# First attention of a two-layer block: scores and maxima as products of 64 rows, the two heads of a pair in turn on the two halves of TensorE's rows

## The reference, cut to what matters

```python
q = query @ w_q                     # layer-normed x, 256 -> 16 heads of 64
k, v = jnp.split(context @ w_kv, 2, axis=-1)
scores = jnp.einsum('bhqd,bhkd->bhqk', q, k) * 64 ** -0.5
attn = jax.nn.softmax(scores, axis=-1)
out = jnp.einsum('bhqk,bhkd->bhqd', attn, v)
return out @ w_out + b_out          # heads side by side, 1024 -> 256
```

## Time and profile before

| What | Value |
|---|---|
| Median of 3 runs | 3254.3 us |
| The profiled execution, its own time | 3254.05 us |
| Its span | 3252.2 us |
| TensorE (PE) busy | 3098.2 us, 95% |
| VectorE (DVE) busy | 2258.3 us, 69% |
| ScalarE (ACT) busy | 1646.5 us, 51% |
| GpSimd (POOL) busy | 1313.5 us, 40% |
| First attention | to about 1900 us of the span |

### The profile page before, as it was taken

How to read it: one execution, slowest core, us unless ns; L and a number is a source line. 1 busy time by engine, 2 the same in 40 slices (tenths; PEclk the granted TensorE clock), 3 DMA queues, 4 the chain that set the end, 5 groups by cost and what they waited for, 6 DMA issues and landing times. The chain is left out here.

```text
span 3252.2 us, 40235 instructions
## 1 busy us (share of the span) xinstructions
PE 3098.2 (95%) x14204; PEld 1885.1 (58%) x14204; DVE 2258.3 (69%) x3655; ACT 1646.5 (51%) x1882; POOL 1313.5 (40%) x617
## 2 busy tenths in 40 slices
PE   6999999999999999999999969799999999999688
PEld 4556656556566565565565546455555555555368
DVE  5765775765766656757646524688888888887779
ACT  3453443443443434534534412365666666576688
POOL 1774774774765756757746723200000000000002
PEclk8999999999999999999999979799999999999798
DMA  8444544463553454544435332323322322322102
GB/s 235 114 113 124 129 123 109 114 158 83 126 146 84 115 138 102 125 123 107 114 104 127 74 107 81 84 40 70 67 52 65 74 50 64 71 50 50 39 13 91
DMA packets 178268, 313.23 MB, mean 96 GB/s; under 512 B 34968, under 2 KB 90080, under 8 KB 178080
## 3 DMA queue, kind: packets, MB, share of 16 engines
q1 hardware_dynamic: 178080, 310.81, 38.7%
HBM read 88.38 MB, written 29.36 MB: 36 GB/s over the span
## 5 line engine op out<-in xcount | busy, mean ns | idle before, releaser
L916 POOL TENSOR_TENSOR a_prob_sum<-a_prob_sum,a_prob 128x1024 f32<-128x1024 f32 x384 | 918.6, 2392 | 56.7 <-POOL a_prob_sum L916 2.2
L627 ACT ACTIVATE a_prob<-a_t 128x1024 f32<-128x1024 f32 x512 | 516.8, 1025 | 644.9 <-PE a_t L444 459.1
L774 DVE TENSOR_REDUCE a_mhalves<-a_m 128x1 f32<-128x512 f32 x1024 | 688.6, 680 | 105.5 <-PE a_m L408 97.6
L1717 ACT ACTIVATE a_prob<-a_t 128x1024 f32<-128x1024 f32 x512 | 497.6, 1025 | 183.9 <-PE a_t L1558 183.1
L1814 DVE TENSOR_REDUCE a_mhalves<-a_m 128x1 f32<-128x512 f32 x807 | 537.8, 686 | 60.9 <-PE a_m L1537 57.2
L451 PE MATMUL a_o<-a_prob,a_v_all 128*64 128x512 f32 x2048 | 493.7, 604 | 0.0
L408 PE MATMUL a_m<-a_kh_n,a_qz 128*128 128x512 f32 x1024 | 415.7, 418 | 8.5 <-DVE a_kl_n L768 3.9
L916 POOL TENSOR_TENSOR a_prob_sum<-a_prob 128x1024 f32<-128x1024 f32 x64 | 153.4, 2397 | 538.1 <-ACT a_prob L627 475.1
L1537 PE MATMUL a_m<-a_vh,a_qz 128*128 128x512 f32 x807 | 336.9, 438 | 10.0 <-DVE x_sb L1896 4.4
L436 PE MATMUL a_t<-a_q_hl,a_k_hh 128*128 128x512 f32 x1024 | 324.4, 398 | 0.4 <-ACT a_prob L627 0.4
L444 PE MATMUL a_t<-a_q_hm,a_k_lm 66*128 66x512 f32 x1024 | 321.4, 395 | 0.0
(11 more groups left out here) (279 smaller groups left out, 4181.8 us busy)
## 6 DMA issues: line engine op xcount, KB each, us to landing
a_k_hh<-a_kh_n SPq DMA_DIRECT2D x256, 256.0 KB, 4.3
a_k_lm<-a_kl_n SPq DMA_DIRECT2D x128, 256.0 KB, 4.8
a_q_hl<-a_qz SPq DMA_DIRECT2D x128, 128.0 KB, 2.3
a_q_hm<-a_qz SPq DMA_DIRECT2D x128, 128.0 KB, 2.4
a_q_hl<-a_ql_n SPq DMA_DIRECT2D x128, 128.0 KB, 2.4
a_vs<-a_vh SPq DMA_DIRECT2D x256, 64.0 KB, 2.4
a_wq<-wq_parts SPq DMA_DIRECT2D x63, 256.0 KB, 2.7
a_wk<-wk_parts SPq DMA_DIRECT2D x63, 256.0 KB, 3.0
```

What stands on the lines that cost most here:

```text
L627: nc.scalar.activation(prob[:, t % RING], ps_t[t % 2][:, :, :], ACT.Exp, scale=SCALE0).then_inc(s_exp, 1)
L774: nc.vector.tensor_reduce(mhalves[:, qt, hd, n:n + 1], ps_m[:, n, :], AX.X, ALU.max).then_inc(s_max, 1)
L916: nc.gpsimd.tensor_tensor(acc, prob[:, (t - 1) % RING] if t == 1 else acc, prob[:, t % RING], ALU.add).then_inc(s_acc, 1)
L1717: nc.scalar.activation(prob[:, t % RB, 2 * j:2 * j + 2, :], ps_t[j][:, :, :], ACT.Exp, scale=SCALE1).then_inc(s_exp, 1)
```

## The change

All scores and maxima become products of 64 rows. Head 0 takes rows 0 to 63 of the array, head 1 rows 64 to 127, and the program alternates between them (`turn` keeps the alternation over the maxima that stand among the tiles). A tile is now 8 products: for each head high*high, high*low, low*high, and `minus` by `m_rows` (the maxima of both heads, at rows 0 and 64, zeros elsewhere). A maximum product takes one head's 64 rows, heads in turn, and head h uses bank h of `ps_m`. The 16 maxima stay 16. The 12 DMAs of `stack` go, and with them the second copies; SyncE's queue only loads the weights. `split_high_q`, `keep_max_rows` and the query's `split_low` become one instruction each instead of two.

The query projection of `nn` and the maxima's rows go to the two banks of `ps_t[0]` instead of `ps_x`: `project_q` waits for the exponential of tile 6, and the next pair's tile 0 waits in `banks_read` until both banks were read. The order of a pair is new: `probs_v` 4 and 5 follow 2 and 3 at once; `project_q` stands ahead of `max_rows`; the maxima are spread from the pair's begin to after tile 7. `INVERTED_AT` goes from (0, 9, 11, 12) to (8, 10, 10, 12). At the start the split weights get tiles of their own, and GpSimd clears one tile more.

```diff
@@ -128,19 +128,22 @@
         v_all = sb("v_all", [P, KT, H0 * HD0])
-        k_hh = sb("k_hh", [P, 2, 2, NK], F32R)
-        k_lm = sb("k_lm", [P, 2, 2, NK], F32R)
-        q_hl = sb("q_hl", [P, 2, 2, NQ], F32R)
-        q_hm = sb("q_hm", [P, 2, 2, NQ], F32R)
+        k_high = sb("k_high", [P, 2, NK], F32R)
+        k_low = sb("k_low", [P, 2, NK], F32R)
+        q_high = sb("q_high", [P, 2, NQ], F32R)
+        q_low = sb("q_low", [P, 2, NQ], F32R)
+        m_rows = sb("m_rows", [P, 2, NQ], F32R)
+        minus = sb("minus", [P, P], F32R)
+        pieces_k = sb("pieces_k", [P, 4, H0 * HD0], F32R)
+        high_q = sb("high_q", [P, DCH, H0 * HD0], F32R)
+        low_q = sb("low_q", [P, DCH, H0 * HD0], F32R)
         prob = sb("prob", [P, RING, 2, NQ])
         prob_sum = sb("prob_sum", [P, 2, NQ])
         o_raw = sb("o_raw", [P, NQ])
...
@@ -204,16 +206,22 @@
         ctx_weights = ((ctx_high[:], 0, P), (ctx_low[:], 0, P), (ctx_high[:], 1, P),
                        (ctx_tail[:], 2, P), (ctx_tail[:], 3, P))
-        ZEROS = 4
-        STACKS = 16 * 12
+        ZEROS = 5
+        def query_bank(pr):
+            return ps_x[:] if pr.g < 2 else ps_t[0][:, 0, :]
+        def row_bank(pr):
+            return ps_o[:] if pr.g == 0 else ps_t[0][:, 1, :]
         raw_v = oT[:, 0:4, :].rearrange("p (c a) n -> p c (a n)", c=2)
...
-            def stack(nx, loading=None):
...
-                    sp.wait_ge(s_kq, 3 * loading.g - 3)
-                if loading is not None:
-                    load_w(loading, loading.p)
-                sp.wait_ge(s_hi, 3 * nx.g + 2)
-                for hd in range(2):
...
+            def next_weights(pr):
+                sp.wait_ge(s_kq, 3 * pr.g - 3)
+                load_w(pr, pr.p)
             def load_context(b):
                 sp.dma_start(ctx_raw[:, 0, :], d["ctxT"][bass.ds(b, 1), 0:P, :].rearrange("a k n -> k (a n)")
...
                     pe.wait_ge(s_w[u], 32 * (pr.loads - 1 + u))
                     high, low = wq[:, u, 0:DCH, :], wq[:, u, DCH:, :]
-                if pr.g != 0:
-                    pe.wait_ge(s_mkept, 2 * pr.g)
+                bank = query_bank(pr)
+                if pr.g == 1:
+                    pe.wait_ge(s_lo, 1)
+                elif pr.g:
+                    pe.wait_ge(s_exp, KT * (pr.g - 1) - 1)
                 for c in range(DCH):
...
             def max_scores(pr, c):
-                hd, qt, n = c // (MS // 2), c // 2 % QT, c % 2
+                rows, qt, n = half(c % 2), c // 4, c // 2 % 2
                 if c == 0:
-                    pe.wait_ge(s_lo, 3 * pr.g + 3)
+                    pe.wait_ge(s_lo, 2 * pr.g + 2)
                 elif c >= 2:
                     pe.wait_ge(s_max, MS * pr.g + c - 1)
-                pe.matmul(ps_m[:, n, :], qz[:, hd, qt * P:(qt + 1) * P],
-                          kh_n[:, n * 512:(n + 1) * 512], start=True, stop=True).then_inc(s_mx, 1)
+                pe.matmul(ps_m[:, c % 2, :], q_high[rows, pr.set, qt * P:(qt + 1) * P],
+                          k_high[rows, pr.set, n * 512:(n + 1) * 512], start=True, stop=True).then_inc(s_mx, 1)
...
                     pe.wait_ge(s_zero, ZEROS)
-                if pr.g == 0:
-                    pe.wait_ge(s_lo, 2)
-                elif pr.g != 1:
-                    pe.wait_ge(s_rec, QT * (pr.g - 1))
+                if pr.g:
+                    pe.wait_ge(s_exp, KT * pr.g - 1)
                 for qt in range(QT):
-                    mm = pe.matmul(ps_x[0:HD0 + 2, qt * P:(qt + 1) * P], mcol[:, qt, :],
+                    mm = pe.matmul(row_bank(pr)[0:HD0 + 2, qt * P:(qt + 1) * P], mcol[:, qt, :],
                                    ident_r[:], start=True, stop=True)
                 mm.then_inc(s_mrow, 1)
-            def scores(pr, t, among=None):
+            def banks_read(g):
+                pe.wait_ge(s_mkept, g + 1)
+                if g + 1 < B * NP:
+                    pe.wait_ge(s_lo, 2 * g + 3)
+            def scores(pr, t, turn, among=None):
                 u = pr.set
                 keys = slice(t * P, (t + 1) * P)
                 if t == 0:
-                    pe.wait_ge(s_stk, STACKS * (pr.g + 1))
+                    pe.wait_ge(s_lo, 2 * pr.g + 2)
+                    banks_read(pr.g)
                 if t >= 2:
                     pe.wait_ge(s_exp, KT * pr.g + t - 1)
-                for hd in range(2):
-                    pe.matmul(ps_t[t % 2][:, hd, :], k_hh[:, u, hd, keys], q_hl[:, u, hd, :],
-                              start=True, stop=False)
+                def product(weights, moving, turn, start=False, stop=False):
+                    for hd in (turn, 1 - turn):
+                        mm = pe.matmul(ps_t[t % 2][:, hd, :], weights[half(hd), :], moving[half(hd), u, :],
+                                       start=start, stop=stop)
+                    return mm
+                product(k_high[:, u, keys], q_high, turn, start=True)
+                product(k_high[:, u, keys], q_low, turn)
                 if among is not None:
                     max_scores(*among)
-                for hd in range(2):
-                    if t == 0:
-                        pe.wait_ge(s_mkept, 2 * pr.g + 1 + hd)
-                    mm = pe.matmul(ps_t[t % 2][:, hd, :], k_lm[0:HD0 + 2, u, hd, keys],
-                                   q_hm[0:HD0 + 2, u, hd, :], start=False, stop=True)
-                mm.then_inc(s_qk, 1)
+                    turn = 1 - turn
+                product(k_low[:, u, keys], q_high, turn)
+                product(minus[:], m_rows, turn, stop=True).then_inc(s_qk, 1)
...
-            def denominators(pr, nx, nn):
-                if nn is not None:
-                    pe.wait_ge(s_lo, 3 * nn.g + 2)
-                elif nx is not None:
-                    pe.wait_ge(s_mkept, 2 * nx.g + 2)
+            def denominators(pr):
+                if pr.g == 0:
+                    pe.wait_ge(s_lo, 3)
...
+                    return 0 if nx is None else MS - len(todo)
                 def maxima(count):
                     for _ in range(min(count, len(todo))):
                         max_scores(*todo.pop(0))
-                def among():
-                    return todo.pop(0) if todo else None
+                def tile(t, within=0):
+                    turn = taken() % 2
+                    scores(pr, t, turn, todo.pop(0) if todo and within else None)
                 if pr.p == 0:
-                    scores(pr, 0)
-                    scores(pr, 1)
+                    tile(0)
+                    tile(1)
                     if pr.g:
                         pe.wait_ge(s_x, QT * (pr.g // NP))
+                    maxima(1)
+                    tile(2, 1)
+                    maxima(1)
+                    tile(3, 1)
+                    maxima(1)
+                elif pr.p == NP - 1:
+                    tile(0)
+                    maxima(1)
+                    tile(1, 1)
+                    maxima(1)
+                    tile(2, 1)
+                    maxima(1)
+                    tile(3, 1)
+                    maxima(1)
+                else:
                     maxima(2)
-                elif pr.p == NP - 1:
-                    scores(pr, 0)
+                    tile(0)
                     maxima(1)
-                    scores(pr, 1, among())
+                    tile(1)
                     maxima(2)
-                else:
+                    tile(2)
                     maxima(1)
-                    scores(pr, 0)
+                    tile(3, 1)
                     maxima(1)
-                    scores(pr, 1, among())
-                    maxima(1)
-                scores(pr, 2, among())
-                maxima(1)
-                scores(pr, 3, among())
-                maxima(1)
-                scores(pr, 4, among())
-                if pr.p == 0:
-                    maxima(1)
-                scores(pr, 5, among())
-                maxima(1)
                 pe.wait_ge(s_oraw, pr.g)
                 probs_v(pr, 0)
                 probs_v(pr, 1)
+                maxima(2 if pr.p == NP - 1 else 1)
+                tile(4, 1)
+                maxima(1)
+                tile(5, 1 if pr.p == 0 else 0)
                 maxima(2)
                 probs_v(pr, 2)
                 probs_v(pr, 3)
+                if turned is None:
+                    probs_v(pr, 4)
+                    probs_v(pr, 5)
                 maxima(1)
-                scores(pr, 6, among())
+                tile(6, 1 if pr.p == 0 else 0)
                 maxima(1)
-                if pr.p == 0:
-                    scores(pr, 7, among())
-                else:
-                    scores(pr, 7)
-                assert not todo
-                if nx is not None:
+                tile(7, 1)
+                maxima(1)
+                if turned is not None:
+                    maxima(1)
                     max_rows(nx)
-                if turned is not None:
                     turn_queries(turned)
```

(46 more changed lines are left out.)

64 lines of the change are left out of this document (20 added, 44 removed).

## The result

| | before | after |
|---|---|---|
| median of the runs, us | 3254.22 (3253.83 to 3255.27, 4 runs) | 3277.26 (3274.27 to 3279.71, 4 runs) |
| profiled execution, us (span) | 3254.05 (3252.2) | 3277.47 (3275.3) |
| denominators to denominators, middle pair | 24.50 | 24.72 |
| pair 6; pair 7; pair 0 of the next batch | 25.80; 25.18; 57.32 | 26.31; 26.62; 56.20 |

The change makes the kernel slower by 0.7%: ratio 1.007, interval 1.0052 to 1.0087. The forecast was 3212 us, faster. The time lies within its range of 3140 to 3325 us but on the wrong side of no change.

The account below looks back on a forecast made before the run. The prediction took TensorE's issue of products to bound the first attention. Seven batches at -5.1 us and a last at -6.7 made -42 us, from 3254.05 to 3212 us; range 3140 to 3325 us.

Parts of the forecast that it names:

- The new wait: Middle pair: TensorE waits for VectorE's reductions at maxima 10 and 11, 0.4 + 0.5 us, with tile 2's wait 1.0 us.
- The pairing: Products on two row halves run together, 0.12 us each, 80 in 9.6 us against 11.3: gain 1.7 us a pair.
- the rows' wait: TensorE's 0.2 us wait for the maxima's rows goes, since `project_q` now stands ahead of `max_rows`.
- Pair 0: First pair of a batch: only one wait of 0.5 us, and a longer rows' wait goes: -1.7 us.
- Pair 6: Pair with queries turned: extra waits at maxima 12 and 14 and for last reductions and joining: +0.7 us.
- Pair 7: Maxima 7 and 8 issued together; waits of 0.45, 0.9 and 1.8 us at maxima 9, 10 and 12: +0.9 us.
- DMAs: The 12 stacking transfers a pair that go were hidden under TensorE; their removal counted as nothing.
- The small instructions: Three small instructions a pair go on ScalarE and VectorE; covered by TensorE, counted as nothing.
- GpSimd: Its additions have 1.8 to 2 us of room in a pair, so it stays unwaited in middle pairs.
- Rival 2: Row halves do not run concurrently: 80 products at 0.235 us, +7.5 us a pair, 3714 us; chance 0.13.
- Rival 3: Row halves pair only partly, slower from 0.135 us a product; at 0.154 us 3325 us; chance 0.15.
- Rival 1: Row pairs run together without waits at the maxima: 62 pairs at -1.75 us, 3145 us; chance 0.17.

Follow-up runs that it names:

- e12: Kernel after with only inversions 1 and 2 moved from ahead of reduction 10 to ahead of 11, INVERTED_AT (8, 11, 11, 12): 3188.85 us, ratio 0.9796.
- e8: Products of 64 rows without stacking, but pair order and INVERTED_AT (0, 9, 11, 12) of the kernel before: 3203.20 us, ratio 0.9843.
- e1: Kernel after with INVERTED_AT (7, 11, 12, 13) instead of (8, 10, 10, 12): 3183.72 us, ratio 0.9785.
- e4: Kernel after with each reduction cut to 64 of its 512 columns, inversions unmoved: 3181.02 us, ratio 0.9776.
- e5: e1 with 12 DMAs a pair of the removed stacking's sizes put back, into scratch nothing reads: 3183.46 us, ratio 0.9784.
- e6: e1 with `probs_v` in two blocks of four tiles and inversions at (10, 10, 11, 11) in pairs 1 to 5 and 7: 3160.98 us, ratio 0.9709.
- e9: e1 with all products of scores and maxima on rows 0 to 63: 3672.22 us (one run).
- e3: Kernel after with a tile's four products of one head first, then four of the other: 3389.05 us, ratio 1.0413.

## Why the prediction was wrong

**The sign failed on two terms of a middle pair, about equal in size.** The forecast was -1.7 - 0.2 + 1.0, taken as -1.0; measured is -1.33 + 1.55 = +0.22. With either term right the pair would still have come out about 0.35 us shorter (-1.9 + 1.55, or -1.33 + 1.0).

*The new wait, the step that failed in its mechanism.* The prediction says "VectorE is done with reduction 6 at 5.3 and idle until maximum 7's product has ended, 7.3", and puts waits of 0.4 and 0.5 us at maxima 10 and 11. The code has a `maxima(1)` behind `tile(3, 1)` in the middle pairs too; I counted seven maxima ahead of `probs_v` 0 where there are eight. Reduction 7 and inversion 0 thus run beside `probs_v` and cost nothing (DVE 126.75). For the same reason maximum 12, not 11, is the last ahead of `probs_v` 2, and it needs reduction 10, the one behind two inversions. The prediction had worked out exactly this wait for pair 7 (1.8 us at maximum 12); it belongs to all middle pairs. Shown by e12, which moves only those two inversions: 24.72 to 23.16.

*The pairing, right in its mechanism and too large in size.* Forecast 1.9 us with the rows' wait; measured 0.97 alone (e8), 1.33 with the order (e1). The step of 0.117 us in a steady tile is as forecast, and nearly every product has a partner, the maxima too: the one at 124.33 starts with the second product of the line at 124.09. A middle pair of e1 has 41 starts for its 80 products, at 0.232 us 9.5 us. But its three stretches of scores and maxima last 5.24, 2.98 and about 2.6 us, 10.85 in all. Six changes to and from the other kinds of product, 0.6 us, the prediction had counted elsewhere; 0.3 us more lie at the ends of the stretches; and at four places the next two products start 0.33 us later instead of 0.23 (124.56 to 124.89), 0.4 us. Without the six changes that is 10.25 us, 0.128 a product and not 0.12.

At each of the four places TensorE has stopped for a moment: it starts 0.055 to 0.07 us behind the end of what it waits for, which in e1 and in the kernel after is reduction 0, reduction 2, the exponential of tile 1 and reduction 8. So a wait too short to be listed costs 0.1 us behind it. With the short reductions of e4 the steps behind maxima 2 and 10 are 0.22 and 0.23 us. The prediction had 0.1 to 0.2 us at tile 2, where reduction 2 comes just as late, 0.4 at maximum 10 for reduction 8, and nothing at maximum 2 and tile 3.

Of the 1.33 us of e1 only 1.05 lie in these stretches (11.90 us in the kernel before; e8 has 10.93, all of its 0.97). The other 0.28 come from the rest of the pair, for which the prediction had no gain: `probs_v` 2 to 5 take 3.58 us in one block where they took 3.73 in two, and the four products of the maxima's rows 0.24 instead of 0.39.

*The clock, not in the prediction.* I gave no price to what can follow a wait in the granted clock; it is 1.7 us in each of three pairs, 5.2 us.

**Other terms.**

- Pair 0: forecast -1.7, measured -1.12. The size of the pairing would account for it; no run takes this pair apart.
- Pair 6: forecast +0.7, measured +0.51, near by luck. The terms listed for it sum to -1.0 + 0.25 + 0.4 + 1.3 = +0.95, not +0.7. Its waits were to be 1.0 at maxima 10 and 11, 0.65 at 12 and 14 and 1.3 for the rows, 2.95 us; the trace has 1.39 at maximum 12 and 0.54 for the rows, 1.93 us, and the smaller pairing makes up for that. In e1 the pair is still 25.69, 0.11 under the kernel before: 0.52 us for the rows stay, and its denominators now wait for GpSimd in every batch, as here in the seventh:

```profile
1564.85 1.08 PE L460 MATMUL a_x<-a_prob_sum,ones 128*64 128x512 f32 x4 [0.53 <-POOL a_prob_sum L917]
```

- Pair 7: forecast +0.9, measured +1.44, of which the inversions' places are 26.62 - 23.78 = 2.84 and the rest -1.40. The three waits that the prediction lists here sum to 3.15, which with -1.9 makes +1.25, not +0.9; the trace shows 2.4 us of waits, and again a smaller gain from the pairing.
- DMAs: nothing, as forecast (e5). The small instructions that went were not tried by themselves.
- GpSimd: unwaited in middle pairs, as forecast, even at 22.75 us a pair (e6). The prediction passed over pair 6, where the kernel before already waits 0.16 us for it in every batch. In the last two pairs gains are swallowed in the last (21.82 us in both kernels), but the loss in the seventh came through, +1.17.

From the forecast of -42 to the +23.4 of the profiled executions: 40 middle pairs x 1.22 = 49; pair 7, 7 x 0.54 = 3.8; pair 0, 7 x 0.58 = 4.1; pair 6, 7 x -0.19 = -1.3; the clock 5.2; the start and the seventh pair of the last batch 2.6. That is 63 of 65 us.

**The rivals.** Rival 2 (no concurrency, 3714 us) is excluded: e9 is that kernel, and it takes 3672 us. Rival 3 (a product at 0.154 us) is excluded by the step in the steady tile; it would have given a slower kernel for a cause that is not there. Rival 1 (no waits, 3145) describes what the kernel can become: e1 takes 3184 without waits in the middle pairs. Of the 39 us between them 40 x 0.42 = 17 are the pairing's size in middle pairs (1.75 forecast there, 1.33 measured) and 7 x 1.64 = 11 pair 6, with its waits for the rows and for GpSimd; the rest was not taken apart.

The Trainium skill's page "TensorE: Matmul & The Clock Gate", Part 3, gives 3.07x for four row tiles, from which the prediction took an estimate of 0.153 us a product. No run here has four tiles. For two halves the trace shows 0.45 / 0.235 = 1.9x (e9 against the kernel after), and the measurement decides: the page's factor must not be carried over to two halves.

## What to carry to other kernels

When a change makes one engine's stage shorter, list for each consumer the order of its queue against the new order of the producer: which reduction frees which buffer, and what stands ahead of it. A list of places written for the old order is then a tuned number that has to be tuned again; here two inversions one place too early were worth 88 us, nearly four times the measured loss. Count such places off the code, one by one for the commonest case, and not from the neighbouring one; and put a price on every place where the engine has to stop, even for a few hundredths of a us: here 0.1 us each, four in a pair.

## What the runs showed of the hardware that I had not expected

- The order in which the two halves' products stand matters little: alternating (3183.7), always the same head first (3181.5) and in twos (3180.9) agree within their ranges; in fours it costs 0.56 us a pair. Products of one half start ahead of earlier ones of the other half.
- A stop of TensorE that is too short to be listed as a wait still costs 0.1 us: behind it the next two products start 0.33 us later instead of 0.23, in e1 at four places of a middle pair.
- After a wait of 1.39 us TensorE's granted clock fell to 0.50, the 1.2 GHz level, in three pairs of the kernel after, and the 16 instructions behind it took 5.35 us instead of 3.65; after the same wait it stayed at 1.00 in the others. After waits of 1.73 us (e3) it fell in 32 of 40 middle pairs. What decides it in a given pair is open.
